# Splitting the expert weights later, G and half of the output product earlier, and no filling products on PE

## What is computed

```python
h = tok_ref(x, mask, ...)          # embedding + windowed features @ weights, layer norm
h = h + attn_ref(layernorm(h))     # 16 heads of 64: softmax(q k^T / 8) v @ Wo, residual, layer norm
h = h + ffn_ref(layernorm(h))      # 16 experts, top 2: gate, gelu(x w1 + b1) w2 + b2, layer norm
# tok_ref:
combined = concatenate([emb[input_ids], pca_feat @ proj_w + proj_b])
fused = combined @ fus_w + fus_b
```

## Time and profile before

| | us |
|---|---|
| median of 3 runs | 567.58 (567.2 to 567.79) |
| the profiled execution, time | 568.68 |
| its span in the profile | 566.9 |
| busy: PE, DVE, ACT, POOL | 517.8, 453.1, 364.3, 385.9 |
| setup block, up to the loop's first matmul | 61.5 |
| mean granted clock of PE, share of full speed | 0.975 |

### The profile page before, as it was taken

How to read it: one execution, slowest core, us unless ns; L and a number is a source line. 1 busy time by engine, 2 the same in 40 slices (tenths; PEclk the granted TensorE clock), 3 DMA queues, 4 the chain that set the end, 5 groups by cost and what they waited for, 6 DMA issues and landing times. The chain is left out here.

```text
span 566.9 us, 16176 instructions
## 1 busy us (share of the span) xinstructions
PE 517.8 (91%) x6053; PEld 386.9 (68%) x6053; DVE 453.1 (80%) x1014; ACT 364.3 (64%) x771; POOL 385.9 (68%) x512
## 2 busy tenths in 40 slices
PE   4957789999999999999999999739999999999985
PEld 2846557777777777787777777524447776777774
DVE  5797567888888888898888888968855988887776
ACT  1636577878778787787878778514675655555540
POOL 3060625878778787887878778842194977898783
PEclk9997799999999999999999999988999999999999
DMA  6900000000000000000000000000633044063011
GB/s 203 334 2 1 2 2 3 3 3 3 3 3 3 4 2 3 3 3 3 3 3 3 3 3 2 3 0 2 157 82 84 19 110 103 23 147 81 28 41 56
DMA packets 11905, 21.73 MB, mean 38 GB/s; under 512 B 4668, under 2 KB 9780, under 8 KB 10164
## 3 DMA queue, kind: packets, MB, share of 16 engines
q1 hardware_dynamic: 11828, 20.71, 13.3%
HBM read 16.24 MB, written 4.33 MB: 36 GB/s over the span
## 5 line engine op out<-in xcount | busy, mean ns | idle before, releaser
L789 POOL TENSOR_TENSOR s_pl<-s_pf,s_ph 128x512 f16<-128x512 f32 x128 | 146.8, 1157 | 16.4 <-ACT s_ph L881 16.4
L970 DVE TENSOR_REDUCE s_mx<-ps 128x4 f32<-128x512 f32 x128 | 83.7, 676 | 29.8 <-PE ps L1111 29.7
L1524 PE MATMUL ps<-s_xt_all,s_w1s 128*128 128x512 f16 x384 | 89.9, 387 | 0.8 <-PEq L772 0.8
L1547 PE MATMUL ps<-s_w2s,s_hid 128*128 128x256 f16 x768 | 88.9, 273 | 0.0
L875 ACT ACTIVATE s_pf<-ps 128x512 f32<-128x512 f32 x128 | 76.7, 603 | 17.4 <-PE ps L1124 17.4
L1547 PEld LDWEIGHTS ps<-s_w2s,s_hid 128*128 128x128 f16 x768 | 75.0, 98 | 11.0
L881 ACT ACTIVATE s_ph<-s_pf 128x512 f16<-128x512 f32 x128 | 77.2, 637 | 0.0
L1157 PE MATMUL ps<-s_zh,s_cth 128*128 128x256 f16 x256 | 69.9, 273 | 0.0
L1157 PE MATMUL ps<-s_zh,s_ctl 128*128 128x256 f16 x256 | 69.8, 273 | 0.0
L1157 PE MATMUL ps<-s_zl,s_cth 128*128 128x256 f16 x256 | 69.8, 273 | 0.0
L1524 PEld LDWEIGHTS ps<-s_xt_all,s_w1s 128*128 128x128 f16 x384 | 38.1, 99 | 42.5 <-issue 4.4
(11 more groups left out here) (232 smaller groups left out, 1242.3 us busy)
## 6 DMA issues: line engine op xcount, KB each, us to landing
s_rep<-picks SPq DMA_DIRECT2D x14, 512.0 KB, 6.6
s_stage<-in_w SPq DMA_DIRECT2D x2, 1024.0 KB, 14.1
out<-s_ot_a SPq DMA_DIRECT2D x16, 128.0 KB, 2.2
out<-s_lg SPq DMA_DIRECT2D x16, 128.0 KB, 1.7
s_stage<-in_wq SPq DMA_DIRECT2D x1, 1024.0 KB, 4.8
s_stage<-in_wk SPq DMA_DIRECT2D x1, 1024.0 KB, 6.5
s_stage<-in_wv SPq DMA_DIRECT2D x1, 1024.0 KB, 8.1
s_stage<-in_wo SPq DMA_DIRECT2D x1, 1024.0 KB, 10.2
```

The lines of the kernel that those rows point to most:

```text
L789: nc.gpsimd.tensor_tensor(flat(pl[:, b % 2, 4 * j:4 * j + 4, :]), pf[:, j, :], flat(ph[:, b % 2, 4 * j:4 * j + 4, :]), ALU.subtract).then_ ...
L970: nc.vector.tensor_reduce(mx[:, b % 2, c:c + 4], A[ab][:].rearrange("p (h k) -> p h k", h=4), AX.X, ALU.max).then_inc(max_done[hf][ab], 1)
L1524: mm = nc.tensor.matmul(HB[j % NH][:], w1s[:, wp, c, j * P:(j + 1) * P], xt_all[:, GB * g:GB * (g + 1), xp, c, :], start=(k == 0), stop=(k ...
L1547: mm = nc.tensor.matmul(zb[b % 4], hid[:, g % 2, hp, j, t * P:(t + 1) * P], w2s[:, wp, j, :], start=False, stop=(j == NJ - 1 and hp == 1))
```

## The change

Four things are changed.

1. **Weight splits.** The splits of wg and w1 leave POOL's part of the setup. The high part of w1 is made by ACT in the setup, between the subtractions from Wo and the first square root; all of wg and the scaling and low part of w1 are done by POOL at the start of the loop's block, ahead of w2 and b2. `logits` of the first sequence waits for wg's parts.
2. **G and two parts of the output product** (`gram`, `z_part(0)`, `z_part(1)`) stand on PE ahead of `u_cols(0)`; ACT splits G ahead of everything of u, and the load of the exponential's table comes behind that. The banks of the output product are exchanged so that the first two parts don't use G's banks; the wait for G's low parts moves to part 2.
3. **Evacuations of the turned rows.** ACT takes all four banks of each group, DVE none.
4. **Filling products.** All are gone, 63 in the setup and 50 in the loop.

```diff
-        Z_BANKS = [psum[n] for n in (0, 1, 5, 4)]
+        Z_BANKS = [psum[n] for n in (5, 4, 0, 1)]
...
-                pool.wait_ge(in_w12, 48)
-                split(both(wgs[:, 0]), both(wgs[:, 1]), both(wg_f[:]), 0)
-                split(both(w1s[:, 0]), both(w1s[:, 1]), stage2[:, 0, :], 3)
...
+                act.wait_ge(in_w12, 48)
+                nc.scalar.activation(both(w1s[:, 0]), stage2[:, 0, :], ACT.Copy, scale=W_SCALE)
                 root(0, v1, q1)
                 table(1)
                 root(1, v2, q2)
-                nc.scalar.preload_act_table(ACT.Exp)
                 table(2)
...
+                g_hi()
+                nc.scalar.preload_act_table(ACT.Exp)
                 u_hi(0)
                 u_hi(1)
                 u_hi(2)
-                for n in range(3):
+                z_hi(0)
+                for n in range(4):
                     u_cols(0, n)
                 u_hi(3)
-                g_hi()
-                for g in (1, 2):
-                    for n in range(3):
+                z_hi(1)
+                for g in range(1, NQ):
+                    for n in range(4):
                         u_cols(g, n)
-                z_hi(0)
-                z_hi(1)
-                for n in range(3):
-                    u_cols(3, n)
                 z_hi(2)
                 z_hi(3)
...
                 u_lo(1)
-                u_cols(0)
+                z_lo(0)
                 u_rows(3)
...
-                for g in range(1, NQ):
-                    u_cols(g)
-                for n in range(4):
+                for n in range(1, 4):
                     z_lo(n)
...
-                keep_going(8, psum[0][:, 0:FREE])
-                u_cols(0)
                 gram()
-                for g in range(1, NQ):
-                    keep_going(6, psum[5][:, 0:FREE])
+                z_part(0)
+                z_part(1)
+                pe.wait_ge(prod_ok, 2 * NQ)
+                for g in range(NQ):
                     u_cols(g)
-                for n in range(4):
-                    z_part(n)
+                z_part(2)
+                z_part(3)
...
+                def scale_and_lo(hi, lo, full, done):
+                    nc.gpsimd.tensor_scalar(full, full, W_SCALE, 0.0, ALU.mult, ALU.add).then_inc(w_hi, 1)
+                    pool.wait_ge(w_hi, done + 1)
+                    nc.gpsimd.tensor_tensor(lo, full, hi, ALU.subtract).then_inc(w_hi, 1)
+
+                pool.wait_ge(in_w12, 48)
+                nc.gpsimd.tensor_scalar(both(wgs[:, 0]), both(wg_f[:]), W_SCALE, 0.0, ALU.mult, ALU.add).then_inc(w_hi, 1)
+                pool.wait_ge(w_hi, 1)
+                scale_and_lo(both(wgs[:, 0]), both(wgs[:, 1]), both(wg_f[:]), 1)
+                scale_and_lo(both(w1s[:, 0]), both(w1s[:, 1]), stage2[:, 0, :], 3)
                 nc.gpsimd.tensor_scalar(both(w2s[:, 0]), stage2[:, 1, :], W_SCALE, 0.0, ALU.mult, ALU.add).then_inc(w_hi, 1)
...
-                BETWEEN = {(-4, 0): 10, (-4, 1): 6, (-3, 0): 10, (-3, 3): 6, (-2, 0): 10, (-2, 2): 8}
```

More of the change, by code:

```diff
@@ L122, in build @@
         psum = [ctx.enter_context(nc.psum_tensor(f"ps{n}", [P, 512], F32)) for n in range(8)]
-        w_split = sem("w_split")
         in_w12, in_b2 = sem("in_w12"), sem("in_b2")
@@ L182, in build @@
         root_count = [0]
-        uf_ok, uh_ok, ul_ok, ut_ready, ut_ok, ut_last_ok = (sem(n) for n in ("uf_ok", "uh_ok", "ul_ok", "ut_ready", "ut_ok", "ut_last_ok"))
+        uf_ok, uh_ok, ul_ok, ut_ready, ut_ok = (sem(n) for n in ("uf_ok", "uh_ok", "ul_ok", "ut_ready", "ut_ok"))
         qkv_ready, qkv_ok, g_ready, ghi_ok, glo_ok, z_ready, zhi_ok, zlo_ok, wo_step = (
@@ L470, in roots @@
                     then(nc.vector.scalar_tensor_tensor(out=sig[:], in0=v2[:], scalar=1.0 / T_SCALE, in1=r2[:], op0=ALU.mult, op1=ALU.mult))
-                def u_cols(g):
-                    dve.wait_ge(ut_ready, 4 * g + 4)
-                    nc.vector.tensor_copy(ub_b[:, 4 * g + 3, :], UT_BANKS[3][:]).then_inc(ut_last_ok, 1)
                 def u_rows(g):
@@ L521, in _ @@
             def _(pe):
[L522 to L526, removed]
                 pe.wait_ge(in_pp, 48)
@@ L554, in _ @@
                         mm.then_inc(nt_ready, 1)
-                keep_going(19, psum[0][:, 0:FREE])
                 pe.wait_ge(in_id, 16)
@@ L563, in _ @@
                 tp.then_inc(mt_ready, 1)
-                keep_going(6, psum[0][:, 0:FREE])
                 pe.wait_ge(mt_ok, 1)
@@ L609, in u_cols @@
                     for n in range(4):
[L610 to L613, removed]
+                        if g >= 1:
+                            pe.wait_ge(ut_ok, 4 * g - 3 + n)
                         for k in range(2):
@@ L633, in z_part @@
                         pe.wait_ge(qkv_ok, 6)
+                    elif n == 2:
                         pe.wait_ge(glo_ok, len(G_PARTS))
@@ L642, in z_part @@
                     mm.then_inc(z_ready, 1)
-                keep_going(12, psum[0][:, 0:FREE])
                 quads(0)
@@ L827, in x_rows @@
                                             ALU.add, ALU.mult).then_inc(x_done, 1)
+                def scale_and_lo(hi, lo, full, done):
[7 more added lines that the diff above has]
+                scale_and_lo(both(w1s[:, 0]), both(w1s[:, 1]), stage2[:, 0, :], 3)
                 nc.gpsimd.tensor_scalar(both(w2s[:, 0]), stage2[:, 1, :], W_SCALE, 0.0, ALU.mult, ALU.add).then_inc(w_hi, 1)
+                pool.wait_ge(w_hi, 6)
+                scale_and_lo(both(w2s[:, 0]), both(w2s[:, 1]), stage2[:, 1, :], 6)
                 pool.wait_ge(in_b2, 16 * 7)
                 for n, r in enumerate((32, 64)):
-                    pool.wait_ge(w_hi, n + 1)
+                    pool.wait_ge(w_hi, 8 + n)
                     nc.gpsimd.tensor_scalar(b2s[r:r + E, :], b2_f[r:r + E, :], W_SCALE, 0.0, ALU.mult, ALU.add).then_inc(w_hi, 1)
[L834 to L842, removed]
+                pool.wait_ge(w_hi, 10)
+                scale_and_lo(b2s[64:64 + E, :], b2s[64:64 + E, :], b2_f[64:64 + E, :], 10)
+                pool.wait_ge(w_hi, 12)
                 for i in STEPS:
@@ L1081, in token_rows @@
                     mm.then_inc(rows_ready, 1)
[L1083 to L1091, removed]
                 def q_rows(b, hf):
@@ L1175, in logits @@
                     pe.wait_ge(xlo_done, b + 1)
+                    if b == 0:
+                        pe.wait_ge(w_hi, 3)
                     n = 0
@@ L1210, in _ @@
                     tokens(i, 0)
-                    keep_going(i, 3)
                     if has(i + 3):
@@ L1218, in _ @@
                         output(i + 1, 0)
-                    keep_going(i, 2)
                     if has(i + 2):
                         values(i + 2, 0)
-                    keep_going(i, 0)
                     if has(i + 4):
@@ L1231, in _ @@
                         output(i + 1, 1)
-                    keep_going(i, 1)
                     if has(i + 4):
```

## The result

The changed kernel takes 567.87 us by the median of its 22 executions, the kernel before 567.71 (also 22). The changed kernel's executions lie in two groups, eleven from 559.9 to 565.3 us and eleven from 570.5 to 573.3, and the comparison leaves out the upper ones: ratio 0.9908, 95% interval 0.9886 to 0.9929, some 5 us faster. Over all 22 the median has not moved: half of the executions are shorter than the shortest of the kernel before (565.34), and the other half are 3 to 5.5 us above its median. The profiled execution took 564.91 us (span 563.1) against 568.68, and is one of the lower group.

The account below looks back on a forecast made before the run. PE was taken to bound the loop once full, so the change acts through setup and fill: 568.68 -6.3 (setup) +2.1 (fill) +1.5 (clock) = 566.0, less 1.1 for the median: 564.8 us; range 557.8 to 568.3.

Parts of the forecast that it names:

- rival 2: Setup: PE's clock falls too, adding 2.7 us; 567.5 us with the configuration's price (chance 0.16), 560.9 without (0.11).
- Roots, 4.5 gained: Setup, DVE: two root operations no longer held by POOL save 4.8 us, less 0.3 lost on ACT; net 4.5.
- ACT's copy, put at 0.3: Setup, ACT: making w1's high part ahead of the first square root delays that root by 0.3 us.
- G and the table's load ahead of u, 1.05 back: Setup, ACT: G's high parts and the exponential's table load delay the first split of u, giving back 1.05 us.
- Rest of the setup, 2.8 gained: Setup behind the first split of u: ACT takes DVE's evacuations and runs without gaps, gaining 2.8 us more.
- POOL's configuration, 6.9: Loop's start: the configuration of POOL moves there and costs 6.9 us, the middle between 0.02 and 13.8.
- rival 1: Loop's start: POOL's configuration costs nothing to speak of (up to 1.7 us), giving 558.2 us; chance 0.24.
- Clock after the stall, 1.5: Loop fill: PE stands about 6 us before its first values, its clock halves, and 1.5 us are lost.
- Fill without fillers, 3.1 gained: Loop fill on PE: without filling products, score columns start 2.0 us earlier and 1.1 more is saved; 3.1 gained.
- DVE beside POOL in the fill, no term: Loop fill: POOL's longer work does not hold DVE, which reads no two SBUF inputs there; no term.

Follow-up runs that it names:

- e1: The changed kernel with the 19, 6 and 12 filling products at the setup's start put back on PE; 559.32 us, ratio 0.9853.
- e4: The kernel before with all 113 filling products taken out and nothing else changed; 569.28 us, ratio 1.0029.
- e2: The changed kernel with the loop's 50 filling products put back and none in the setup; median 573.55 us of 12 executions, ratio 0.9948.
- e3: e1 with the splits of wg and w1 on POOL in the setup again and ACT's copy of w1 gone; 561.49 us, ratio 0.9886.
- e10: The changed kernel with only the 12 filling products right ahead of the first quads put back; 561.06 us, ratio 0.9885.

## Why the prediction came out as it did

The total was right and the sum was not. 566.0 was forecast for the profiled execution, 564.91 came. The setup came 7.2 us later than predicted, the fill 7.6 shorter with its clock term, the rest 0.7 shorter: two errors of about the same size and opposite sign. That the total came within 1.1 us is luck. For the median 564.8 was forecast; it is 567.87 over all executions and 561.94 in the lower group, near neither. What happened is nearest to rival 2 without a price for the configuration, at 560.9 and a chance of 0.11.

- **Roots, 4.5 gained: right in kind, and conditional.** The two held operations take 0.2 us. The interval from the first root step to u is 4.9 us instead of 9.6. With the clock early (e1) the roots end at 36.7, as predicted. ACT's copy, put at 0.3, costs under 0.1 there: the first root step itself came 0.2 later than before (31.83), and the root follows at 32.12, 0.11 behind its end, where in the changed kernel, with the copy long done, it follows 0.03 behind. In the changed kernel itself the gain wasn't there, since the late quads no longer meet POOL (e4).
- **G and the table's load ahead of u, 1.05 back: right.** In e1 the split starts at 38.87, predicted 38.5: 0.4 more is given back.
- **Rest of the setup, 2.8 gained: right, somewhat small.** From the first split to the loop's opening e1 takes 15.9 us, before 19.4: 3.5 gained. So e1's loop opens at 54.80, predicted 55.15. ACT sets the setup's end, with one low part of DVE behind it.
- **The clock in the setup (rival 2): wrongly weighed and wrongly sized. This is the step that failed.** It was given 0.27 and 2.7 us; it happened, and costs 7.5 us in the profile, more in the executions like e2's. I argued that PE had stood 1.7 us at 52 without losing its clock. But here the clock had not yet risen when the pauses began, and in e2, where it had (11.58), it fell in them. And I took the way back as short, "5.7 us after PE had set out again" as at 67.2. Here the rise came 12.0 us behind the start of the quads, with PE busy throughout, and in e2 28.5 us behind it. So not only quads and tables of 5.5 us ran slowly, but all products up to 34.93.
- **POOL's configuration, 6.9: wrong.** The gap from the configuration to the first arithmetic is about 0.1 us; rival 1 was right here. Between 0.02 and 13.8 I took the middle because no row was nearer. But the upper bound held a wait for a DMA, so it said nothing of the price, and the rows of 11 ns did. The Trainium skill, GPSIMD Engine Reference, section 2.1 Instruction dispatch, has about 6 us for a first call to freshly loaded code; in this trace a TENSOR_SCALAR behind the configuration doesn't pay it. Two roundings in the sum are 0.1 off: 19.0 less 17.2 leaves POOL 1.8 us of slack and not 1.7, and 566.0 less 1.1 is 564.9.
- **Clock after the stall, 1.5:** no stall, no term.
- **Fill without fillers, 3.1 gained: right, somewhat small.** 4.0 in the profile, of which 0.5 is the clock's earlier return and not the fillers'. The score columns came 2.9 us earlier and not 2.0: the first score rows, put at 1.6 earlier, started 2.2 earlier, 0.5 of it by the clock.
- **DVE beside POOL in the fill, no term: right.** The low part of q takes 0.69 us beside POOL's splits, as in the earlier trace rows.

What stays open: why some executions get the clock early and others don't, with the same program. The upper group's cause is shown in e2's profile and inferred for the changed kernel. What the 26 fillers of the setup's second half were worth was not tried.

## What to carry to other kernels

Filling products pay where an engine behind PE waits for it and PE's clock would not be up: here 12 of 113, right ahead of the first dense stretch, bring 6.8 of the 8.6 us between the medians of the changed kernel and e1, and the 50 in the loop's fill cost, by the profiles. No run took the 12 out and left the others in. Take each group out alone before taking all. A gain that rests on two engines meeting at a certain moment (a hold, a wait) is there only as long as the change doesn't move that moment; ask what the other parts of the change do to it. And where two rows bound a price, ask whether the wider one measures the price at all.

## What the runs showed of the hardware

- Ahead of the first change of clock in a trace the clock column says 1.00 and is not to be trusted: 32 products took 7.09 us there and 3.79 at a shown 1.00 in e1. Compare durations of one shape.
- A PE that is busy need not get its clock back: in e2 it stayed at 1.2 GHz for 30.7 us with PE busy for 29.3. In e10 twelve fillers stood right ahead of the rise.
- POOL's configuration at the start of a block costs about 0.1 us before TENSOR_SCALAR: 62.3 to 62.41 in the changed kernel, 54.8 to 54.91 in e1.
- A DVE TENSOR_SCALAR or TENSOR_TENSOR of 0.2 us on 128x32 that starts beside a POOL instruction of 2048 columns can end with that instruction: 1.74 and 3.41 us in the earlier trace rows, 1.14 and 3.92 in e3, each within 0.05 us of POOL's end. A RECIPROCAL beside the same instructions took its 0.35 us (at 33.72 before, at 31.67 in e3), and q's low part its 0.69. The Trainium skill, GPSIMD Engine Reference, section 1 Specifications, has the SBUF interfaces of the two shared; these rows show one small operation waiting out the rest of the large one.
